# Transposing gathered rows by a DMA transpose on ACT's queue in place of TensorE and copies out of PSUM

## The reference

```
x = x + attention1(layernorm(x))     # over the batch, with 64x64 scores
x = x + attention2(layernorm(x), ctx)  # 32 heads, 8 key/value groups, head size 128, RMS norm of q and k
x = x + ffn(layernorm(x))
...
def ffn(x):                          # 16 experts of inner width 256, 4 per token, and a shared one
    scores = sigmoid(x @ gate_w.T) + bias
    topk_w, topk_idx = top_k(scores, 4); topk_w /= sum(topk_w)
    out = sum over the 4 experts of (silu(x @ Wg.T) * (x @ Wu.T) * topk_w) @ Wd.T
    return out + silu(x @ Sg.T) * (x @ Su.T) @ Sd.T
```

## Time and profile before

| | |
|---|---|
| median of 3 runs | 910.18 us (909.82 to 911.87) |
| profiled execution | 911.49 us, its span 909.7 us |
| PE (TensorE) busy | 814.6 us, 90% of the span |
| DVE / ACT / POOL busy | 60% / 56% / 57% |
| mean granted TensorE clock | 0.962 of full speed |
| DMA, over the span | 157 GB/s |
| HBM read, written | 97.85 MB, 41.68 MB |

### The profile page before, as it was taken

The page is one execution under the profiler, slowest core; times in us unless marked ns, Lnnn a source line. Parts: engine busy times, 40 slices in busy tenths (PEclk is TensorE's granted clock), DMA queues, the critical chain, the costliest instruction groups (busy, mean ns, idle before and its releaser), DMA issues.

```text
span 909.7 us, 19207 instructions
## 1 busy us (share of the span) xinstructions
PE 814.6 (90%) x6747; PEld 443.9 (49%) x6747; DVE 548.5 (60%) x1029; ACT 507.3 (56%) x1000; POOL 520.5 (57%) x444
## 2 busy tenths in 40 slices
PE   6689699999999999999999996999699999999930
PEld 2654345545546446446446454445355555555510
DVE  5897577577676765866866864988622222222218
ACT  3778686585684775775775873454034444444410
POOL 6843558859858957957867878132334444344310
PEclk9899899999999999999999998999799999999975
DMA  8055515434425335245245146531345757755248
GB/s 304 3 114 187 186 64 175 156 117 141 137 115 167 110 136 164 92 157 161 74 180 170 43 135 203 220 116 48 128 151 186 247 194 248 262 178 193 93 181 327
DMA packets 51705, 142.45 MB, mean 157 GB/s; under 512 B 6336, under 2 KB 8384, under 8 KB 47296
## 3 DMA queue, kind: packets, MB, share of 16 engines
q1 hardware_dynamic: 43536, 116.93, 38.2%
q0 software_dynamic: 7520, 24.65, 7.9%
q10 hardware_dynamic: 592, 0.08, 0.1%
HBM read 97.85 MB, written 41.68 MB: 153 GB/s over the span
## 4 chain that ended last, share of the span: by engine, by line
PE 63%; DVE 14%; POOL 11%; issue 6%; DMA 3%; ACT 2%; SPq 0%; POOLq 0%; DVEq 0%
PE ps L1492 31%; POOL reg_h L582 5%; PE ps L1914 5%; PE ps L1915 5%; PE ps L1916 5%; POOL reg_h L578 4%; PE ps L1680 2%; DVE x_res L1481 2%; PE ps L1893 2%; PE ps L1937 2%; PE ps L1939 2%; PE ps L1938 2%; POOL ring_mem L527 2%; PE ps L1667 2%; PE ps L1647 1%
## 5 line engine op out<-in xcount | busy, mean ns | idle before, releaser
L1492 PE MATMUL ps<-wo_hi,reg_b 128*128 128x512 f16 x448 | 144.5, 384 | 8.7 <-DVE ring_mem L1129 8.7
L582 POOL TENSOR_TENSOR reg_h<-reg_h 128x512 f16<-128x512 f32 x88 | 109.9, 1259 | 38.0 <-ACT reg_h L803 33.3
L1492 PE MATMUL ps<-hT_hi,wq_hi 128*128 128x512 f16 x256 | 97.7, 381 | 17.2 <-DVE ring_mem L1120 17.2
L609 POOL DMA_INDIRECT y_rows<-reg_h,to_row x47 | 46.4, 987 | 114.8 <-ACT reg_h L977 114.8
L541 POOL TENSOR_TENSOR ring_mem<-kv,ring_mem 128x512 f16<-128x512 f32 x64 | 81.7, 1281 | 52.6 <-ACT ring_mem L737 52.6
L578 POOL TENSOR_SCALAR reg_h<-reg_h 128x512 f32<-128x512 f32 x56 | 92.0, 1643 | 27.9 <-ACT reg_h L801 27.9
L1492 PE MATMUL ps<-hT_lo,wq_hi 128*128 128x512 f16 x256 | 97.5, 381 | 0.0
L1492 PE MATMUL ps<-hT_hi,wq_lo 128*128 128x512 f16 x256 | 97.5, 381 | 0.0
L1492 PE MATMUL ps<-wo_lo,reg_b 128*128 128x512 f16 x224 | 85.9, 384 | 0.0
L1492 PEld LDWEIGHTS ps<-wo_hi,reg_b 128*128 128x128 f16 x448 | 44.1, 98 | 65.3 <-issue 11.0
L1458 DVE SCALAR_TENSOR_TENSOR reg_h<-ps,reg_h 128x256 f32<-128x256 f32 x47 | 20.0, 425 | 91.6 <-ACT reg_h L965 70.7
(11 more groups left out here) (286 smaller groups left out, 2010.9 us busy)
## 6 DMA issues: line engine op xcount, KB each, us to landing
w_split<-reg_h SPq DMA_DIRECT2D x96, 256.0 KB, 2.3
ring_mem<-w_split SPq DMA_DIRECT2D x16, 1536.0 KB
reg_h<-in_wgu SPq DMA_DIRECT2D x64, 256.0 KB, 3.7
stage<-in_wq SPq DMA_DIRECT2D x8, 1024.0 KB, 6.6
stage<-in_wo SPq DMA_DIRECT2D x8, 1024.0 KB, 4.9
reg_h<-in_wd SPq DMA_DIRECT2D x32, 256.0 KB, 3.1
ring_mem<-y_rows SPq DMA_DIRECT2D x8, 1024.0 KB, 13.0
wkv_st<-in_wkv SPq DMA_DIRECT2D x8, 512.0 KB, 7.3
```

The source lines that it names most:

```text
L582: pool.tensor_tensor(hl[:, 1, :], st, hl[:, 0, :], ALU.subtract).then_inc(pre_split, 1)
L609: pool.indirect_dma_start(y_rows, bass.IndirectOffsetOnAxis(ap=to_row[:, r - 1:r], axis=0), y[r % 2], None).then_inc(scattered[r % 2], 16)
L1492: last = pe.matmul(dst, lhsT(c), rhs(c), start=(m == 0), stop=(m == n - 1))
```

## The change

One DMA transpose per tile takes a gathered tile of 128 rows x 1024 fp16 (256 KB) from `h_slot[r % 4]` to `tT[r % 4]`, from SBUF to SBUF. It is issued on ACT's queue, for tile r+3 behind the silu of tile r, and for tiles 1 to 3 ahead of the loop. `tT` has four buffers now. ACT's order becomes silu r, transpose r+3, zT hi r, output copy r-1: the last two changed places. TensorE's eight transposes, ACT's and DVE's copies and the fp16 identity are gone. POOL's gather r+4 waits for the landed transpose of tile r. Some semaphores of loads are merged: mask, norm, gate and bias into one (waits of 80), the shared expert's two into one (waits of 32). Each transpose buffer has a semaphore of its own.

```diff
-        ident_h = sb("ident_h", [P, P], F16)
...
-        tT = [w.bitcast(F16).rearrange("p (z k s) -> p z k s", z=2, k=KC) for w in pair(reg_h[:, 0:1024], 512)]
+        tT_rows = [reg_h[:, 512 * i:512 * i + 512].bitcast(F16).rearrange("p (c s) -> p c s", s=P) for i in range(KC)]
+        tT = [w.rearrange("p (z k) s -> p z k s", z=2) for w in tT_rows]
...
-        tT_ps, tT_hi_done, tT_lo_done = sem("tT_ps"), sem("tT_hi_done"), sem("tT_lo_done")
+        transposed = [sem(f"transposed{i}") for i in range(KC)]
...
+        def lap_of(r):
+            return (r + KC - 1) // KC
...
-            sp.dma_start(wgu_st, wgu[SHARED]).then_inc(wgu_in, 16)
-            sp.dma_start(wd_st, wd[SHARED]).then_inc(wd_in, 16)
+            sp.dma_start(wgu_st, wgu[SHARED]).then_inc(shared_in, 16)
+            sp.dma_start(wd_st, wd[SHARED]).then_inc(shared_in, 16)
...
-            pool.wait_ge(mask_in, 32)
+            pool.wait_ge(small_in, 80)
...
-                    pool.wait_ge(tT_ps, r)
+                    pool.wait_ge(transposed[r % KC], 16 * lap_of(r))
                     pool.nop(nofuse=True)
                     gather(r + KC)
...
-            act.wait_ge(small_in, 48)
+            act.wait_ge(small_in, 80)
...
-                    act.wait_ge(wgu_in, 16)
+                    act.wait_ge(shared_in, 32)
...
-                    act.wait_ge(wd_in, 16)
+                    act.wait_ge(shared_in, 32)
...
-            def slots_hi(r):
-
-                act.wait_ge(tT_ps, r)
-                act.activation(tT[r % 2][:, 0, :, :], ps[:, 4, 0:D // 2].bitcast(F16).rearrange(
-                    "p (k s) -> p k s", k=KC), ACT.Copy).then_inc(tT_hi_done, 1)
+            def transpose_slots(r):
+
+                act.wait_ge(gathered[r % KC], 16 * lap_of(r))
+                act.dma_start(tT_rows[r % KC], h_slot[r % KC].bitcast(F16), transpose=True).then_inc(
+                    transposed[r % KC], 16)
...
-            slots_hi(1)
+            for r in range(1, KC):
+                transpose_slots(r)
             for r in range(1, TILES + 1):
                 gated(r)
-                if r < TILES:
-                    slots_hi(r + 1)
+                if r + KC - 1 <= TILES:
+                    transpose_slots(r + KC - 1)
+                gated_hi(r)
                 if r >= 2:
                     down_out(r - 1)
-                gated_hi(r)
             down_out(TILES)
...
-            slots_lo(1)
             for r in range(1, TILES + 1):
                 gated_up(r)
-                if r < TILES:
-                    slots_lo(r + 1)
                 gated_lo(r)
...
             def gate_up(r, at, loads):
                 pe.wait_ge(ready, loads)
-                pe.wait_ge(tT_hi_done, r)
-                pe.wait_ge(tT_lo_done, r)
+                pe.wait_ge(transposed[r % KC], 16 * lap_of(r))
...
-                hi, lo = tT[r % 2][:, 0, :, :], tT[r % 2][:, 1, :, :]
+                hi, lo = tT[r % KC][:, 0, :, :], tT[r % KC][:, 1, :, :]
...
-            transpose_slots(1)
             shared_down(7)
...
                 gate_up(r, now[0], now[1])
                 if r < TILES:
                     ahead = weights_of(r + 1)
-                    transpose_slots(r + 1)
```

More of the change, by code:

```diff
@@ L260, in decoder_kernel @@
         xy_in = [sem(f"xy_in{j}") for j in range(NT)]
-        ctx_in, mask_in, small_in = sem("ctx_in"), sem("mask_in"), sem("small_in")
+        ctx_in, small_in = sem("ctx_in"), sem("small_in")
         wq_in, wkv_in, wo_in = sem("wq_in"), sem("wkv_in"), sem("wo_in")
-        wgu_in, wd_in = sem("wgu_in"), sem("wd_in")
+        shared_in = sem("shared_in")
         pre_in, pre_stored = ([sem(f"{name}{i}") for i in range(SLOTS)] for name in ("pre_in", "pre_stored"))
@@ L633, in _ @@
             act.preload_act_table_set("natural_log_exp_and_others")
-            act.dma_start(mask_sb[0:S, :], mask).then_inc(mask_in, 16)
-            act.dma_start(mask_sb[S:P, :], mask).then_inc(mask_in, 16)
+            act.dma_start(mask_sb[0:S, :], mask).then_inc(small_in, 16)
+            act.dma_start(mask_sb[S:P, :], mask).then_inc(small_in, 16)
             act.dma_start(norm_sb[:, :], qk_norm).then_inc(small_in, 16)
@@ L649, in _ @@
             act.activation(blockmask16[:, :], blockmask[:, :], ACT.Copy).then_inc(masks16, 1)
-            act.activation(ident_h[:, :], ident[:, :], ACT.Copy).then_inc(masks16, 1)
             def normalise_rows(count, dst, done):
@@ L1108, in _ @@
             row_scales(2, 0)
-            dve.wait_ge(small_in, 48)
+            dve.wait_ge(small_in, 80)
             dve.tensor_tensor(wqk[:, :], norm_sb[:, 0:1], norm_sb[:, 1:2], ALU.mult).then_inc(dve_consts, 1)
@@ L1447, in _ @@
             dve.tensor_reduce(wk[:, :, :], wk_cmp[:, :, :, :], AX.X, ALU.add).then_inc(wk_done, 1)
[L1449 to L1452, removed]
             def gated_up(r):
@@ L1500, in _ @@
             pe.wait_ge(consts, 14)
-            pe.wait_ge(masks16, 3)
+            pe.wait_ge(masks16, 2)
             def keep_clock(n):
@@ L1882, in _ @@
                 shared_down(t)
[L1885 to L1895, removed]
             def weights_of(r):
```

## The result

The changed kernel takes 949.48 us in the median of four runs (941.65 to 957.81) against 910.99 of the kernel before on the same chip: a ratio of 1.037 (95% interval 1.031 to 1.043), slower, where 889.6 was forecast. Every ratio, with its interval, leaves out executions more than 1.5% above the fastest of their kernel (here the 957.81), so it is not quite the quotient of the two medians. The profiled execution is the fastest of the four, 941.65 us with a span of 939.8, 30.1 longer than the span before.

The account below looks back on a forecast made before the run. TensorE was taken to bound the expert loop. From the profiled 911.49 us, -19.6 in the loop, -4.0 at its start and +3.0 for bursts gave 890.9, or 889.6 against the median; range 884 to 896, chance 0.70.

Parts of the forecast that it names:

- what the change takes off TensorE: Expert loop: eight slot transposes leave TensorE, 0.44 us a tile, 20.5 us over 46 tiles.
- z's lost cover: Expert loop: without the transposes, the fp32 weight load waits slightly for z, charged 0.02 us a tile, 0.9 us.
- the bursts: Expert loads fill the DMA engines and delay gathers that ACT waits for: 0 to 24 us possible, 3 us taken.
- the sign that the prediction set for rival 1: ACT idle on gathers for microseconds in many tiles would show the prediction wrong.
- rival 1: Every expert load stalls ACT behind a late gather, 22 us in place of 3, result about 908; chance 0.10.
- the price on the DMA engines: Each transpose's time on the 16 DMA engines: 1.3 us taken, loop sum 181 us in about 195, fitting on the whole.
- rival 4: DMA becomes the bound: gain shrinks past 1.6 us a transpose, loss past 2.1, about 1056 at 5.2; chance 0.06.
- the loop's start: Gate/up of tile 1 no longer waits for DVE's lo copy: up to 5.4 us gained, 4.0 taken.
- the issue on ACT: Issuing a transpose holds ACT's sequencer 1 to 2 us a tile, about 2.7 being free; cost taken as nothing.
- rival 2: The issue holds ACT: at 4.8 us, 75 us more, about 985; a loss from 3.2 us on; chance 0.09.
- rivals 3 and 5: Eight transpose blocks go in series, about 1550 us, chance 0.03; or the wait for z eats the gain, chance 0.02.
- Rival 5: Transposes leave TensorE but the wait for z takes their whole place, gaining nothing; chance 0.02.

Follow-up runs that it names:

- e1: Changed kernel with POOL issuing each gather one tile earlier: 926.98 us, ratio 1.013.
- e5: Changed kernel without 11 of the 12 expert loads, their tiles using stale weights: 901.71 us, ratio 0.991.
- e7: Changed kernel with gathers one tile earlier and a plain DMA copy in place of the transpose: 899.71 us, ratio 0.990.
- e4: Changed kernel with a plain DMA copy of the same 256 KB in place of the transpose, same queue and place: 916.25 us, ratio 1.003.
- e12: Changed kernel with e10's and e9's edits, only the lo half transposed by DMA, the hi half by TensorE: 902.87 us, ratio 0.991.
- e9: Kernel before, on DVE tile 1's lo copy ahead of the last shared addition and token weights behind the loop: 906.48 us, ratio 0.993.
- e2: Changed kernel with the transpose issued behind the output copy on ACT: 962.02 us, ratio 1.052.
- e8: Kernel before plus one 256 KB DMA transpose a tile behind the silu on ACT's queue, result not read on TensorE's path: 934.10 us, ratio 1.026.
- e10: Changed kernel with gathers one tile earlier and each expert load in three 512 KB pieces, each issued after the last landed: 917.32 us.
- e6: Changed kernel with gathers one tile earlier and each expert load in six 256 KB pieces, each issued after the last landed: 965.40 us.

## Why the prediction was wrong

**Right: what the change takes off TensorE.** 4.54-4.10 = 0.44 us a tile was forecast and is there in every tile that does not stall; z's lost cover cost TensorE nothing that can be seen.

**Wrong, and the largest: the bursts.** The step said "TensorE stalls if it takes over about 6 us", priced a stall at up to 2.2 us in each of 11 loads, and took 0.3 each, 3 us. They cost 51. Two things were off. The landing of a gather was in no row; the step judged it by the scatters, of which one was past 7.0 us. It was 5.0 in the median and 11.5 at most, under the changed kernel's own load. And the stalls were counted as single events, though the prediction itself names the queue behind the wait: output copy, scatter, next gather. That is a ring. The chain has 4.24 us from the start of ACT's issue to the start of the next gather (736.88 to 741.12), and to that comes the gather's landing. TensorE needs a lap of two tiles in 8.2 us, so a landing may take 3.96 us. This is the 4.0 after which "ACT wants it"; the 2 us more, up to 6, can be used up once, and come back only by gathers that land in under 4.0. At the median landing a lap is 9.2 us, and the slack does not come back. e1, e5 and e7 bear this out, and the sign that the prediction set for rival 1 came, ACT idle on gathers in 16 tiles. Rival 1 named the wait, had a chance of 0.10 and a price of 22 us, less than half of what came. (The 2.2 us has no working; 8.9-6 from its own rows would give 2.9, and 32 us.)

**Wrong: the price on the DMA engines.** "I take 1.3" from the one row of a move inside SBUF; it is 1.70 us. The prediction's own rival 4 put the edge at 1.6. The sum was 120+61 = 181 us; the share in the windows adds up to 0.80x45+0.92x136+0.87x37+0.53x32 = 210 us, since gathers and scatters took longer as well: their queue went from 7.9% of 909.7 us to 9.1% of 939.8, 72 to 86 us. The price is not a constant either: 8.4% of 903.4 us without the loads (e5), 1.61 us a tile, and 11.1% of 935.3 in e1, 2.21 us. e4 and e7 put 27 to 33 us on engine time and issue together, and e12 shows that half of the engine time can be borne.

The Trainium skill (DMA: Bandwidth & Descriptors, Latency and other measured facts) has 261 GB/s for a DMA transpose with non-contiguous middle dimension, 1.0 us as an estimate; here 256 KB in 1.70 us are 154 GB/s. The Trainium skill's sentence that trn2's transpose DMAs are as fast as regular ones (Advanced Engine Details and Errata, X-Bar Transpose (TRN2)) does not hold here: 1.70 against 0.70 us. The Trainium skill's table (VectorE: DVE Perf Modes, The three transpose paths), with 390 ns for a block on TensorE and 1309 ns by DMA, had the side right, though not the size: eight blocks by DMA land in 3.1 us or more.

**Wrong: the loop's start.** 4.0 us were forecast, "since the transpose has 7 us"; none came. The 7 us had to hold the landing of gather 1 too, which started at 643.33 and let ACT issue at 647.95, 4.6 us later. From there to gate/up at 655.71 are 7.8 us, with four gathers and an expert load on the same DMA engines (POOL's next gather, which waits for the same transpose, starts at 656.25). The plain copies of e4 took as long, from 647.03 to gate/up at 654.71; so it was the load there, and not the transposing. e9 shows that the hole was worth about 6 us, and that it could be had by DVE's order alone. Its granted clock stays at 1.00 from 648 to 660, where it was 0.64 in 656 to 660 before.

**Right in size, wrong in "Cost: nothing": the issue on ACT.** 1.25 us in the median lies in the 1 to 2 us taken, below the 2.7 from which it was to cost. That limit holds when the gather is there. Behind a late gather the issue is a link of the ring from its first microsecond, and it has 10.1% of the chain over the loop. Four issues in the loop took over 2.7 us, the longest 4.47, and 15.2 in e2, so rival 2's mechanism came up as a consequence of the load. In e8, where a copy that TensorE needs stands behind it, 1.25 us of issue cost 0.5 us a tile on the mean.

**Right: rivals 3 and 5 stayed away.** The eight blocks do not go one after another at 2.3 us each: a transpose lands in 3.1 us at the least, 3.9 in the median. Rival 5 is refuted by the 4.10.

**Open.** Of the 27 to 33 us of the transpose's price, how much is engine time and how much is issues made long by full engines was not separated; no run changed one without the other. Why small pieces of a transpose take 2.4 times the engine time of 2 KB rows, whether by the pieces' size or by the transposing itself, was not separated either. Nor was the reason for the wide spread of some kernels. It does not go with the transposes as such: e4 and e7, with plain copies, lie 19 and 11 us apart over 10 and 6 runs, e10 29 over 13 and the kernel before 13 over 23 in the same job, but e8, with transposes and a DMA share of 0.95, only 2 over 4.

## What to carry to other kernels

Before work is moved from a full engine to the DMA queues, add up the DMA time in the stage, the moved work at its own rate (short pieces, not bytes), and ask for room in bursts, not on the mean. Draw the new wait as a graph: if what is queued behind it leads back to the transfer that it waits for, the time of one lap (every link, and the landing under load) divided by the tiles in a lap is a bound of its own. Slack can be used up only once in such a ring. Then issue the transfer ahead of everything that depends on the waiting engine, look what stands behind each issue in its queue, and look first for a hole that an order alone can close.

## What the runs showed of the hardware

A DMA transpose of 128 x 1024 fp16 from SBUF to SBUF makes 1056 packets of 248 B on the mean (50224 less the 592 of other small loads, over 47). It takes 1.70 us of all 16 DMA engines in the changed kernel (1.61 to 2.21 in other runs) where a plain copy of the same bytes takes 0.70, holds the issuing queue for 1.25 us (0.47 for the copy) and lands in 3.1 to 12.5 us. Under a full load the issue was held up to 15.2 us. Gathers of 256 KB beside loads and transposes landed in 3.2 to 11.5 us, 5.0 in the median. An expert load of 1.5 MB in six pieces, one in flight, took 29 us beside the transposes (698.6 to 727.8 in e6) and 17 us after the last of them (914.6 to 931.5), where the whole load at once lands in 8.4 us in the median of the changed kernel.
